# A perceiver's attention values, selective scan, long attentions, adapters, expert places and gates written anew in a hand-ordered kernel

## What is computed

```python
# block 0: attention, 16 heads of 8, 128 keys per head;   block 4: causal, 16 groups per sequence
attn = softmax(q @ k.T * scaling);  out = attn @ v
# block 1: selective scan over 128 tokens, N = 16 states of 128 channels
dA = exp(dt_t[..., None] * A);  h = dA * h + (dt_t * u_t)[..., None] * B_t[:, None, :]
y = einsum('bdn,bn->bd', h, C_t)          # with Bt = u @ W_B, Ct = u @ W_C
# block 3: one head of 8, 2048 keys, masked;   block 6: one head of 128, 2048 keys
attn = softmax(where(mask, -1e9, q @ k.T / sqrt(d)));  out = attn @ v
# block 5: of 8 adapters the one with the least reconstruction loss
mid = relu(x @ Wd + bd);  out = x @ W_base + b_base + mid @ Wu + bu
# block 8: 16 experts with a capacity
locations = cumsum(mask, axis=0) - 1;  dispatch = einsum('tec,td->ecd', sec_mask, tokens)
# block 11: 16 experts, 4 gated per token, and a shared one
y = y + c_e[:, None] * ((silu(gate) * up) @ w2_e.T)
```

## Time and profile before

| | us |
|---|---|
| median of 3 runs | 1203.15 |
| the runs | 1201.7, 1203.15, 1211.84 |
| the profiled execution | 1213.89 |
| its span | 1211.8 |
| block 1, of the span | 118.7 to 192.7 |
| block 9, of the span | 607.5 to 1141 |

### The profile page before, as it was taken

The page is one execution under the profiler, slowest core; times in us unless marked ns, Lnnn a source line. Parts: engine busy times, 40 slices in busy tenths (PEclk is TensorE's granted clock), DMA queues, the critical chain, the costliest instruction groups (busy, mean ns, idle before and its releaser), DMA issues.

```text
span 1211.8 us, 14434 instructions
## 1 busy us (share of the span) xinstructions
PE 1112.2 (92%) x5448; PEld 653.1 (54%) x5448; DVE 575.7 (48%) x1003; ACT 426.5 (35%) x705; POOL 312.6 (26%) x93
## 2 busy tenths in 40 slices
PE   6999689997899988879979999999999999999888
PEld 4666334665666655758955444444444444443754
DVE  3887774236477643145173443443443434343444
ACT  3664413325387542321144223223232332223111
POOL 0000000000000000000003666656655665566000
PEclk9999889999999999997889999999999999999899
DMA  8200000020000020060000000000000000000200
GB/s 344 108 1 1 1 0 1 1 110 31 2 1 1 17 88 1 1 260 1 1 1 5 22 17 21 15 18 17 22 14 18 22 18 18 15 20 5 77 1 9
DMA packets 21371, 40.07 MB, mean 33 GB/s; under 512 B 2496, under 2 KB 18880, under 8 KB 19648
## 3 DMA queue, kind: packets, MB, share of 16 engines
q1 hardware_dynamic: 21312, 39.25, 8.8%
HBM read 38.98 MB, written 0.26 MB: 32 GB/s over the span
## 4 chain that ended last, share of the span: by engine, by line
PE 55%; DVE 5%; ACT 4%; issue 1%; POOL 1%; POOLq 0%; DVEq 0%
PE PSUM L2017 18%; PE PSUM L2021 18%; PE PSUM L1930 2%; PE PSUM L2149 1%; PE PSUM L2064 1%; PE PSUM L1536 1%; PE PSUM L1579 1%; PE PSUM L1949 1%; ACT ARENA L623 1%; POOL RSTD L379 1%; PE PSUM L1471 1%; PE PSUM L2163 1%; PE PSUM L1958 1%; PE PSUM L1464 1%; PE PSUM L2155 1%
## 5 line engine op out<-in xcount | busy, mean ns | idle before, releaser
L435 POOL TENSOR_TENSOR ARENA<-ARENA 128x2048 f32<-128x2048 f32 x64 | 288.9, 4514 | 176.6 <-ACT ARENA L708 176.6
L1312 DVE TENSOR_TENSOR ARENA<-PSUM,RK 128x512 f32<-128x512 f32 x256 | 176.2, 692 | 281.4 <-PE PSUM L2017 278.9
L2017 PE MATMUL PSUM<-ARENA,CK 128*128 128x512 f32 x512 | 252.8, 596 | 0.7 <-ACT ARENA L704 0.7
L2021 PE MATMUL PSUM<-ARENA,CK 128*128 128x512 f32 x512 | 251.2, 593 | 2.1 <-ACT ARENA L708 2.1
L708 ACT ACTIVATE ARENA<-ARENA,CK 128x2048 f32<-128x2048 f32 x64 | 128.2, 2003 | 313.0 <-DVE ARENA L1312 313.0
L2021 PEld LDWEIGHTS PSUM<-ARENA,CK 128*128 128x128 f32 x512 | 96.7, 190 | 126.5 <-issue 107.9
L2017 PEld LDWEIGHTS PSUM<-ARENA,CK 128*128 128x128 f32 x512 | 96.6, 191 | 118.8 <-issue 97.6
L379 POOL TENSOR_TENSOR RSTD<-VE,MHALF 128x4 f32<-128x4 f32 x15 | 15.1, 1009 | 478.3 <-DVE VE L790 478.3
L1498 PE MATMUL PSUM<-WK,CT 128*128 128x512 f32 x256 | 124.4, 608 | 0.3 <-ACT SQ L465 0.3
L811 DVE TENSOR_REDUCE RK<-SQ 128x8 f32<-128x512 f32 x128 | 84.8, 682 | 34.5 <-ACT SQ L465 34.3
L1471 PE MATMUL PSUM<-WA 128*128 128x128 f32 x626 | 83.1, 286 | 12.9 <-DVE VE L790 9.4
(11 more groups left out here) (391 smaller groups left out, 1250.4 us busy)
## 6 DMA issues: line engine op xcount, KB each, us to landing
CT<-in_ctxT SPq DMA_DIRECT2D x4, 1024.0 KB, 9.9
CK<-in_l0f_experts SPq DMA_DIRECT2D x1, 4096.0 KB, 22.6
CK<-in_ctxk SPq DMA_DIRECT2D x1, 4096.0 KB, 13.6
ARENA<-in_l2f_experts SPq DMA_DIRECT2D x2, 2048.0 KB, 8.3
CK<-in_ctxT SPq DMA_DIRECT2D x64, 64.0 KB, 1.7
CK<-in_ctxr SPq DMA_DIRECT2D x64, 64.0 KB, 1.8
ARENA<-in_l2f_experts SPq DMA_DIRECT2D x1, 3072.0 KB, 14.4
WB<-in_wb SPq DMA_DIRECT2D x1, 2834.5 KB, 11.0
```

The lines of the kernel that those rows point to most:

```text
L435: nc.gpsimd.tensor_tensor(LS[b % 2], LS[b % 2], PR[:, k % 2, :], ALU.add)\
L1312: ve.tensor_tensor(PR[:, k % 2, c * 512:(c + 1) * 512].rearrange("p (j n) -> p j n", j=4), PSUM[:, c % 2, :].rearrange("p (j n) -> p j n", ...
L2017: mm(bank(c % 2), CTT[:, k, :], qpb[:, b, c * 512:(c + 1) * 512], start=True, stop=True)\
L2021: return mm(bank(4 + c), CKT[:, k, :], PR[:, k % 2, c * 512:(c + 1) * 512], start=first, stop=final, skip_group_check=True)
```

## The change

1. Blocks 0 and 4: each quad of value matmuls now loads 32 columns of V (the head's 8 and 24 that nobody reads) and streams 128 columns of PT, in four column tiles of bank 6 (`sum_values`). After four heads ScalarE copies bank 6 to OT (`keep_values`), TensorE turns it in four transposes into bank 0 (`turn_values`), and VectorE takes 16 reciprocals and multiplies 128 columns (`scale_values`), three times inside the loop and once behind it. `stay_busy(8)` and `stay_busy(5)` behind the loops go.
2. Block 1: four quarters of 2048 in place of two halves; the scan's states use two halves of DA and HS in turn. B and C rows are computed once, in four column tiles, and copied by VectorE to BC; a spread is then a matmul of 32 rows, in four row tiles in turn. The products overwrite HS. The keys of block 3 are computed between the quarters, and `busy_until_variance` stands at block 2's start in their place.
3. Blocks 3 and 6: three banks (4, 5, 7) take turned chunks; scores of a later sequence stand between the turns and the sums, and each chunk's sums follow its copy. The arena's regions KT, VX, KEEP, NEG are moved.
4. Block 5: the relu goes from ScalarE to VectorE; the base matmuls stand ahead of the losses, the bias matmuls and the up matmuls go out as each mask lands; less `stay_busy`.
5. Block 6: the offset matmuls stand behind the first scores. 6. Block 8: places by 4 matmuls of 64, 48, 32 and 16 columns; the comparison in two parts of 1280 elements; `stay_busy` 18 becomes 7; `turn_placed(0)` ahead of `first(1)`. 7. Block 11: gates of two pairs at a time in two row tiles, turned by 8 matmuls of 32 columns in place of 4 transposes.

```diff
+    def keep_values(g):
+        nc.scalar.wait_ge(sem("values_summed"), g + 1)
+        act(OT[:, :], bank(6), ACT.Copy).then_inc(sem("pt_ready"), AC.sends("pt_ready"))
...
-            last = act(DA[:, n * 512:(n + 1) * 512], DT, ACT.Exp, scale=ANEG[:, half * 8 + n:half * 8 + n + 1])
...
+    for q in range(4):
...
+            nc.scalar.wait_ge(sem("l0a_scan"), due)
+        for n in range(4):
+            at = (q % 2 * 4 + n) * 512
+            last = act(DA[:, at:at + 512], DT, ACT.Exp, scale=ANEG[:, q * 4 + n:q * 4 + n + 1])
         last.then_inc(sem("l0a_decay"), AC.sends("l0a_decay"))
...
+        if q:
+            context_keys_act(q - 1)
+    context_keys_act(B - 1)
...
-        if n % 2:
-            k = n // 2
-            nc.scalar.wait_ge(sem("l1f_hidden"), AC.due("l1f_hidden"))
-            act(MID[:, k, :], bank(1 + k % 2), ACT.Relu, bias=w("l1f_bdown")[:, k:k + 1])\
-                .then_inc(sem("l1f_hidden_kept"), AC.sends("l1f_hidden_kept"))
...
+    def scale_values(k, signal, n=1):
...
+        nc.vector.wait_ge(sem("v_rows"), DV.due("v_rows"))
...
+        ve.reciprocal(L_INV[:, some], L_SUM[:, some]).then_inc(sem("dve_step"), DV.sends("dve_step"))
...
+        ve.tensor_tensor(ACC[:, :, :].rearrange("p b (h e) -> p h b e", h=H)[:, 4 * k:4 * k + 4, :, :],
+                         PSUM[:, 0, :].rearrange("p (h b w) -> p h b w", h=4, b=B)[:, :, :, 0:HD],
+                         L_INV[:, some].rearrange("p (h b) -> p h b", h=4).unsqueeze(3).broadcast_to([P, 4, B, HD]),
+                         ALU.mult).then_inc(sem(signal), DV.sends(signal, n))
...
+        if h > 4 and h % 4 == 1:
+            nc.vector.wait_ge(sem("probs_totalled"), DV.sent("probs_totalled"))
+            scale_values(h // 4 - 1, "v_kept")
...
-    for half in range(2):
-        for n in range(8):
+    for q in range(4):
+        half = slice(q % 2 * 2048, (q % 2 + 1) * 2048)
...
+            ve.tensor_tensor(DBU[:, at:at + 512], bank(SPREAD_BANKS[(q * 8 + n) % 6]), DTU, ALU.mult)\
...
-        ve.tensor_tensor_scan(HS, DA, DBU, 0.0, ALU.mult, ALU.add).then_inc(sem("l0a_scan"), DV.sends("l0a_scan"))
+        if q >= 2:
+            nc.vector.wait_ge(sem("l0a_added"), 4 * (q - 1))
+        ve.tensor_tensor_scan(HS[:, half], DA[:, half], DBU, 0.0, ALU.mult, ALU.add)\
+            .then_inc(sem("l0a_scan"), DV.sends("l0a_scan"))
...
+            ve.tensor_tensor(HS[:, at:at + 512], HS[:, at:at + 512], bank(SPREAD_BANKS[(q * 8 + 4 + n) % 6]), ALU.mult)\
...
+        if b >= 2:
+            nc.vector.wait_ge(sem("long_turned"), 4 * (b - 1))
...
+        if n % 2:
...
+            ve.tensor_scalar(MID[:, k, :], bank(1 + k % 2), w("l1f_bdown")[:, k:k + 1], 0.0, ALU.add, ALU.max)\
...
-        last = ve.tensor_tensor(m, m, each(SHALF[:, :, k], P), ALU.mult)
-    last.then_inc(sem("l1f_masked"), DV.sends("l1f_masked"))
+        ve.tensor_tensor(m, m, each(SHALF[:, :, k], P), ALU.mult).then_inc(sem("l1f_masked"), DV.sends("l1f_masked"))
...
-    ve.tensor_tensor(PLACED.rearrange("p (a c) -> p a c", c=ROOM), each(GATE, ROOM),
-                     over(slots, B * 16), ALU.is_equal)\
...
+    for s in range(2):
...
+        ve.tensor_tensor(placed, place.unsqueeze(3).broadcast_to([P, B, 8, CAPACITY]),
+                         slots[:, 0:CAPACITY].unsqueeze(1).unsqueeze(1).broadcast_to([P, B, 8, CAPACITY]), ALU.is_equal)\
...
+    def sum_values(g, v_of):
...
+        nc.tensor.wait_ge(sem("pt_ready"), PE.due("pt_ready", n=2 if g and g % 4 == 0 else 1))
+        for j in range(4):
+            last = mm(PSUM[32 * j:32 * j + 32, 6, (g % 4) * P:(g % 4 + 1) * P], v_of(g, j),
+                      PT[:, g % 2, j * P:(j + 1) * P], start=True, stop=True)
+        last.then_inc(sem("values_summed"), PE.sends("values_summed"))
...
+    def turn_values(k):
...
+        if k:
+            nc.tensor.wait_ge(sem("v_kept"), PE.due("v_kept"))
+        for j in range(4):
+            last = tp(PSUM[:, 0, j * P:(j + 1) * P], OT[:, j * P:(j + 1) * P], ident)
...
+        def turn_chunk(b, c):
...
+                last = tp(PSUM[:, TURNED_BANKS[k], j * P:(j + 1) * P], SL[:, b % 2, t * P:(t + 1) * P], ident)
...
+        def sum_chunk(b, c):
+            nc.tensor.wait_ge(sem("long_pt"), PE.due("long_pt"))
...
+                    last = mm(PSUM[32 * j:32 * j + 32, 6, 0:P], VX[:, b, j, 32 * c:32 * c + 32],
+                              PTL[:, 4 * c + j, :], start=c == 0, stop=c == 3)
+                else:
+                    last = mm(PSUM[:, 6, 0:P], CK[:, b * KEY_TILES + 4 * c + j, :], PTL[:, 4 * c + j, :],
...
+            nc.tensor.wait_ge(sem("long_probs"), PE.due("long_probs"))
+            if not masked and b + 1 < B:
+                scores(b + 1)
+            for c in range(3):
+                turn_chunk(b, c)
+            sum_chunk(b, 0)
+            turn_chunk(b, 3)
+            if masked and b + 1 < B:
                 nc.tensor.wait_ge(sem("long_scores_taken"), PE.due("long_scores_taken"))
-            else:
...
-            for c in range(4):
-                due = PE.due("long_pt", lag=2)
...
-                    last = tp(PSUM[:, 4 + c % 2, j * P:(j + 1) * P], SL[:, b % 2, t * P:(t + 1) * P], ident)
...
-                for j in range(4):
-                    for c in range(4):
-                        last = mm(PSUM[32 * c:32 * c + 32, 6, 0:P], VX[:, b, j, 32 * c:32 * c + 32],
-                                  PTL[:, 4 * c + j, :], start=j == 0, stop=j == 3)
...
+                if b + 2 < B:
+                    scores(b + 2)
+            for c in range(1, 4):
+                sum_chunk(b, c)
...
-            at = (B * h + b) * HD
-            last = mm(PSUM[:, 6, at:at + HD], PT[:, h % 2, b * P:(b + 1) * P], VS[:, at:at + HD], start=True, stop=True)
-        last.then_inc(sem("values_summed"), PE.sends("values_summed"))
-    stay_busy(8)
+        sum_values(h, lambda g, j: VALUES[:, (B * g + j) * HD:(B * g + j) * HD + 32])
+        if h and h % 4 == 0:
+            turn_values(h // 4 - 1)
+    nc.tensor.wait_ge(sem("pt_ready"), PE.due("pt_ready"))
+    turn_values(3)
...
+    for j in range(4):
+        last = mm(PSUM[32 * j:32 * j + 32, 4, :], w("l0a_WBC"), U, start=True, stop=True)
+    last.then_inc(sem("l0a_product"), PE.sends("l0a_product"))
...
-        mm(bank(SPREAD_BANKS[k % 6]), w(name)[:, n:n + 1].broadcast_to([P, P]), U, start=True, stop=True)\
...
+        r = 32 * (k % 4)
+        mm(bank(SPREAD_BANKS[k % 6]), ident[r:r + 32, r + n:r + n + 1].broadcast_to([32, P]), BC[r:r + 32, :],
+           start=True, stop=True).then_inc(sem("l0a_bc"), PE.sends("l0a_bc"))
...
+    def add_state(q, n):
...
+        nc.tensor.wait_ge(sem("l0a_bc_taken"), 8 * q + 4 + n + 1)
...
-    for half in range(2):
-        for k in range(22 * half, 16 * half + 14):
-            spread(k)
-        for n in range(8):
-            add_state(half, n)
-            if 16 * half + 14 + n < 32:
-                spread(16 * half + 14 + n)
-    stay_busy(4, 3)
...
+    for k in range(8):
+        if k == 6:
...
+        spread(k)
+    context_keys_pe(0)
+    for q in range(4):
+        if q < 3:
+            for n in range(4):
+                if q == 0 and n == 2:
+                    stay_busy(5, 1)
+                spread(8 * (q + 1) + n)
+        for n in range(4):
+            add_state(q, n)
...
+            for n in range(4):
+                spread(8 * (q + 1) + 4 + n)
+            context_keys_pe(q + 1)
+    stay_busy(4)
...
-    nc.tensor.wait_ge(sem("x_ready"), PE.due("x_ready", n=2))
...
+    busy_until_variance(3, 6, 5)
...
-    stay_busy(8)
+    for b in range(B):
+        sl = slice(b * P, (b + 1) * P)
+        mm(PSUM[:, 6, sl], HT[:, sl], w("l1f_Wbase"), start=b == 0, stop=False, skip_group_check=True)
+    stay_busy(4)
     nc.tensor.wait_ge(sem("l1f_losses"), PE.due("l1f_losses", n=NA))
     mm(PSUM[:, 5, 0:32], w("ones"), SM[:, 0:32], start=True, stop=True).then_inc(sem("l1f_loss"), PE.sends("l1f_loss"))
-    stay_busy(20)
+    stay_busy(12)
...
         sl = slice(b * P, (b + 1) * P)
-        mm(PSUM[:, 6, sl], HT[:, sl], w("l1f_Wbase"), start=True, stop=False)
-        for k in range(4):
+        mm(PSUM[:, 6, sl], PICKT_(b), w("l1f_bup", NA), start=False, stop=False, skip_group_check=True)
+    for k in range(4):
+        nc.tensor.wait_ge(sem("l1f_masked"), PE.due("l1f_masked"))
+        for b in range(B):
+            sl = slice(b * P, (b + 1) * P)
             last = mm(PSUM[:, 6, sl], MID[:, k, sl], w("l1f_Wup")[:, k * P:(k + 1) * P],
-                      start=False, stop=False)
...
-    for b in range(B):
-        for c in range(b + 1):
-            last = mm(PSUM[:, 6, b * 16:(b + 1) * 16], w("upto") if c == b else w("ones"),
...
+    mm(PSUM[:, 6, 0:4 * 16], w("upto"), LG, start=True, stop=False, skip_group_check=True)
+    for c in range(B - 1):
+        later = B - 1 - c
+        last = mm(PSUM[:, 6, (c + 1) * 16:B * 16].rearrange("p (b e) -> p b e", b=later), w("ones"),
```

(21 more changed lines are left out.)

239 lines of the change are left out of this document (126 added, 113 removed).

## The result

| | before | after |
|---|---|---|
| median, us | 1203.2 (4 runs) | 1163.43 (4 runs) |
| the runs, us | 1201.7 to 1211.84 | 1162.53 to 1167.67 |
| profiled execution, us | 1213.89 | 1163.65 |
| its span, us | 1211.8 | 1161.9 |

A forecast was written before the change was run, and what follows sets the result against it. No single bound was taken: each block was priced by the wait ending last, TensorE's 92% being no proof. Gains of 4.3, 11.8, 0, 2.4, 5.7, 4.8, 4.5 and 3.0 sum to 36.5, taking 1203.15 to 1166.6 us (own range 1158 to 1175, wider 1150 to 1184).

The forecast's parts named there:

- a quarter is VectorE's 9.33: Block 1: VectorE's products, half scan and small gaps take 9.33 us a quarter, so four quarters end at 174.3.
- the last adds: Block 1's end: four adds at 0.885 each end about 1.3 us after the products, about 3.5 later still at lower clock.
- the sign: Block 1: first product to last read of bank 1 about 40.5 us, with VectorE idle under 3 us.
- Rival A: Block 1: row tiles don't overlap, a spread costs 0.885; 6.9 us worse than forecast, 1173.5; chance 0.10.
- D: Block 1, rival: TensorE at its lower clock throughout, 37 us lost where 11.8 are forecast, 1215.4; chance 0.03.
- The saving per head: Blocks 0 and 4: a quad of values with its gaps costs 0.57 or 0.53 us, not 0.78, saving 0.25.
- only the groups without the ScalarE wait gain in full: Block 4: only the eight groups where TensorE doesn't wait for ScalarE's squares can gain, 8 × 0.25; block total 1.0 us.
- the charge of 1.3 for the three turns: Blocks 0 and 4: three added turns of four transposes in the loop, 0.42 us each, deducted as 1.3.
- Rival C: Blocks 0 and 4: tiles pay no gap, a quad costs 0.20 us; 11.7 better than forecast, 1154.9; chance 0.10.
- rival B: Blocks 1, 5 and 6: work now on the path runs at half clock rate, costing 12.1 us, 1178.7; chance 0.15.
- the gather waits for 1280 of 4096 elements: Block 8: with the comparison split, the gather waits only for its first part, 3.0 us gained.
- The 0.9 deducted for it: Block 11: 0.9 us taken off the 4.2 saved on gates, for ScalarE's and VectorE's first use of both banks.

## Why the prediction was right, point by point

**Block 1, 11.8 forecast, 11.3 measured.** The step "a quarter is VectorE's 9.33" held to 0.04 wherever TensorE had its clock (9.37 in after, and all three intervals in three other traces). The wait on the last adds came out at 2.00. In seven of the ten traces with row tiles one of the three intervals is 9.9 to 10.9, each with a granted clock of 0.50 in part of it; the prediction had put half of that cost on the last adds alone. VectorE is idle for 3.7 of the 40.96, where under 3 had been named as the sign. Rival A is refuted by the 1.14 for four spreads and priced by the run with one row tile; it would have cost more than the 6.9 worked out, because with it comes a part of D.

**Blocks 0 and 4, 4.3 forecast, 7.3 measured.** The mechanism was right, and two terms of the sum were mis-sized. The saving per head was put at 0.25 and is 0.34 (4.77 to 4.43, 6.05 to 5.71). In block 4 the step that only the groups without the ScalarE wait gain in full held: the six long ones in the loop gain 0.34 each, the short ones without a turn 0.01 to 0.09, but for the last with 0.34. What was wrong is the charge of 1.3 for the three turns. They stand in short groups, which take 4.82 with a turn and 4.68 with only the wait, so a turn costs 0.14 there and not 0.42: it fills time in which TensorE would wait for ScalarE. The 0.24 at 404.62 in the earlier trace rows cost nothing before (loads beside it are 0.24 apart without any wait); only with shorter quads does ScalarE set the pace of these groups. Rival C, no gap at all, is refuted: the row at 78.92 has its 0.20 of idle.

**Blocks 3 and 6, 7.2 forecast, 7.2 measured,** by luck: where the clock is alike the order gains 2.6 and 5.4, so 8.0, and the lower clock takes 1.7 of it in block 3 and adds 0.9 in block 6. In block 6 a period gained 1.17, not 1.0, and the last wait 1.85 of the 1.8 forecast, which makes 5.4 where the clock is alike; in that, the offset brings the first exponential 0.4 sooner (15.2 after the block's start for 15.6), costed at nothing, and the first period gives as much back. In block 3 the order gives 2.6 from the second exponential on (2.4 forecast), but on the mean of the traces only 0.9 arrives, since a part of the block is at the lower clock in each of them (2.09 for the first scores in after). That is rival B in one place, in an amount that changes between executions.

**Block 5, 5.7 and 5.6.** The X add was forecast at 450.95, a wait of 2.7; it is 3.03, and the loop gave 1.5 for 1.3.

**Block 8, 4.5 and 5.5.** The wait went from 3.80 to 0.97 (forecast 1.5), since the four matmuls ran mostly at the full clock, where the ten of before had gone to the lower one half way. But the step "the gather waits for 1280 of 4096 elements" was wrong, before and after: the last to end is TensorE's filler, 0.82 after the comparison in before and 0.65 after its first half in after. What was gained is that filler of seven matmuls ends sooner than filler of eighteen; that the sum came within 1.0 is in part luck. How much of the 5.5 the shorter filler would give alone was not tried.

**Block 11, 3.0 and 2.1.** The gates save 1.05 four times, but `down` of the even pairs now waits for VectorE's product behind the late gate (the two pairs take 7.04, of which TensorE works 6.7). The 0.9 deducted for it was too small: two pairs gain 0.68 (7.72 less 7.04), not 1.05.

**Rival B, the clock,** was given 12.1 us and came only in small part: with filler cut in blocks 5, 6 and 8 these blocks have 1.00, 1.00 and 0.97 in after, and the adds of block 1 lose 1.2 in one quarter. The reader of one trace sees a cost of the clock in block 8 of before (8 us) and in block 3 of after (2 to 4 us). The first is chance: two other traces of that form don't have it. Of the second the amount is chance, and whether the new form always brings some of it is open. That the median came out 3.3 better than forecast is the values of blocks 0 and 4 (3.0 more) for the most part; the other misses add up to 0.5 less, and the 0.8 between the table's 39.0 and the 39.8 of median is within the scatter of the medians (1203.2 and 1206.8 for the kernel before).

## What to carry to other kernels

Price a block from the engine that would pace it with all waits gone, and check that the others fit under it also at TensorE's lower clock: four row tiles made that room here, 9.4 to 10.9 us a quarter with them and 11.9 to 15.7 without. Where matmuls have few rows or few columns, rebuild them so that neighbours fall into different tiles, and group them, since a quad of column tiles among full-width matmuls showed about 0.2 us of idle behind it here (0.17 ahead and 0.20 behind in the earlier trace rows). Look also at what filler ends: it was the filler, not the comparison, that let block 8's gather start. Before explaining a block by the clock, take a second trace of the same kernel.

## What the runs showed that was not expected

- TensorE's lower clock wanders: in two traces of one kernel block 3 had 0.83 and 0.92 and block 1 0.92 and 0.82, in two of the kernel before block 8 had 0.81 and 0.94. With more filler it stood in other blocks, and with less filler block 1 had 0.81, no lower than the 0.82 of the changed kernel.
- The kernel before varies more than the changed one: 1199.6 to 1216.6 in 17 runs, against 1162.5 to 1167.7 in the eight of the changed kernel. Why was not tried.
- The loops of blocks 0 and 4 repeat to 0.03 us between executions in the old form (79.20 to 79.23) and to 0.01 in block 0's new form (75.27 and 75.28), and to 0.18 in block 4's new form, where ScalarE paces some groups (76.58 to 76.76). The same blocks as a whole differ by up to 3, and block 0's start by 4: a loop's length inside a block is the better measure of a part.
